# A selective-scan kernel on Trainium2: loops written out, softplus parts added on TensorE, five items read out by GpSimd, step rows replicated first

## The reference

```python
def mamba_block(seq, in_proj_w, conv_w, conv_b, x_proj_w, dt_proj_w, dt_proj_b, A_log, D, out_proj_w):
    xz = jnp.einsum('bld,ed->ble', seq, in_proj_w)
    u, z = jnp.split(xz, 2, axis=-1)
    ...
    u = jax.nn.silu(u)
    x_dbl = jnp.einsum('bld,ed->ble', u, x_proj_w)
    dt, Bm, Cm = jnp.split(x_dbl, [DT_RANK, DT_RANK + D_STATE], axis=-1)
    dt = jax.nn.softplus(jnp.einsum('blr,dr->bld', dt, dt_proj_w) + dt_proj_b)
    A = -jnp.exp(A_log)

    def step(h, inputs):
        dt_t, B_t, C_t, u_t = inputs
        dA = jnp.exp(dt_t[:, :, None] * A)
        h = dA * h + (dt_t * u_t)[:, :, None] * B_t[:, None, :]
        y = jnp.einsum('bdn,bn->bd', h, C_t)
        return (h, y)
    ...
    y = ys.transpose(1, 0, 2) + u * D
    y = y * jax.nn.silu(z)
    return jnp.einsum('bld,ed->ble', y, out_proj_w)
```

## Time and profile before

| | |
|---|---|
| median of 3 runs | 1939.89 us (1939.37 to 1941.07) |
| the profiled execution, its own time | 1938.45 us |
| its span | 1936.7 us |
| busy, share of the span | PE 80%, ACT 51%, DVE 66%, POOL 63% |
| DMA | 311.06 MB, mean 161 GB/s |
| scans of layer 0 (first to last gate) | 73.3 to 578.1 us |
| scans of layer 1 (first to last gate) | 1095.8 to 1602.2 us |

### The profile page before, as it was taken

The page is one execution under the profiler, slowest core; times in us unless marked ns, Lnnn a source line. Parts: engine busy times, 40 slices in busy tenths (PEclk is TensorE's granted clock), DMA queues, the critical chain, the costliest instruction groups (busy, mean ns, idle before and its releaser), DMA issues. The chain is left out here.

```text
span 1936.7 us, 25492 instructions
## 1 busy us (share of the span) xinstructions
PE 1546.9 (80%) x6220; PEld 927.2 (48%) x6221; DVE 1271.6 (66%) x2146; ACT 991.2 (51%) x1594; POOL 1211.5 (63%) x1179
## 2 busy tenths in 40 slices
PE   5677777777778998999982687777777777699996
PEld 3222222222228998989981222222222227566664
DVE  5799999999996531111115799999999996411012
ACT  4777777777772211222223777777777772122112
POOL 2699999999981001444435699999999992123310
PEclk8799999999995899999995799999999995599997
DMA  5788777787774204777765877788877881423313
GB/s 131 191 183 185 181 179 177 176 186 179 178 160 155 85 25 143 233 220 218 226 162 134 206 179 176 179 182 179 181 176 174 184 186 49 171 78 122 123 62 107
DMA packets 104507, 311.06 MB, mean 161 GB/s; under 512 B 19389, under 2 KB 74509, under 8 KB 93069
## 3 DMA queue, kind: packets, MB, share of 16 engines
q1 hardware_dynamic: 91896, 291.72, 60.1%
q0 software_dynamic: 12544, 18.63, 4.1%
HBM read 258.83 MB, written 51.45 MB: 160 GB/s over the span
## 5 line engine op out<-in xcount | busy, mean ns | idle before, releaser
L689 POOL TENSOR_TENSOR mamba_dbu<-mamba_rep 128x462 f32<-128x462 f32 x640 | 677.2, 1085 | 66.1 <-DMA mamba_rep<-dt_rows 66.1
L509 PE MATMUL mamba_ysum<-mamba_hc,all_sel 128*128 128x462 f32 x800 | 379.4, 588 | 148.3 <-DVE mamba_hc L797 147.3
L621 ACT ACTIVATE mamba_state<-mamba_rep,all_m_acol 128x462 f32<-128x462 f32 x640 | 388.9, 638 | 156.6 <-DVE mamba_last L808 155.6
L811 DVE TENSOR_TENSOR_SCAN mamba_state<-mamba_state,mamba_carry,mamba_dbu 128x462 f32<-128x462 f32 x400 | 455.4, 1179 | 0.0
L509 PEld LDWEIGHTS mamba_ysum<-mamba_hc,all_sel 128*128 128x128 f32 x800 | 130.3, 190 | 398.3 <-DVE mamba_hc L797 318.8
L808 DVE TENSOR_TENSOR_SCAN mamba_last<-mamba_state,mamba_last,mamba_dbu 128x462 f32<-128x462 f32 x240 | 280.3, 1168 | 15.2 <-POOL mamba_dbu L689 12.4
L684 POOL TENSOR_TENSOR mamba_hcp<-mamba_last,mamba_rep 128x462 f32<-128x462 f32 x240 | 266.7, 1111 | 5.6 <-DVE mamba_last L808 5.6
L504 PE MATMUL mamba_ysum<-mamba_hcp,all_sel 128*128 128x462 f32 x480 | 227.8, 570 | 50.1 <-POOL mamba_hcp L684 50.0
L797 DVE TENSOR_TENSOR mamba_hc<-mamba_state,mamba_rep 128x462 f32<-128x462 f32 (+1 forms) x240 | 230.7, 961 | 0.0
L1433 DVE TENSOR_TENSOR moe_h<-moe_sg,moe_up 128x512 f32<-128x512 f32 x62 | 42.6, 688 | 283.0 <-PE moe_up L1242 276.6
L504 PEld LDWEIGHTS mamba_ysum<-mamba_hcp,all_sel 128*128 128x128 f32 x480 | 85.3, 190 | 172.4 <-POOL mamba_hcp L684 119.6
(11 more groups left out here) (236 smaller groups left out, 2285.6 us busy)
## 6 DMA issues: line engine op xcount, KB each, us to landing
mamba_rep<-bc_rows SPq DMA_DIRECT2D x168, 462.0 KB, 7.4
mamba_rep<-dt_rows SPq DMA_DIRECT2D x168, 462.0 KB, 7.5
weights_wgu<-in_L_gu_dram SPq DMA_DIRECT2D x88, 512.0 KB
dt_rows<-mamba_dd SPq DMA_DIRECT2D x168, 115.5 KB, 7.2
weights_w<-in_L_w_dram SPq DMA_DIRECT2D x16, 1024.0 KB
mamba_xs<-seq_scratch SPq DMA_DIRECT2D x92, 116.0 KB, 9.2
seq_scratch<-mamba_y SPq DMA_DIRECT2D x40, 116.2 KB, 7.0
normed_rows<-xn SPq DMA_DIRECT2D x16, 288.0 KB, 7.1
```

The source lines that it names most:

```text
L509: nc.tensor.matmul(ysum[:, 0:TC], sel[:, i // NM, :], hc[:, n % HCD, :], start=False, stop=end).then_inc(hc_summed, 1)
L621: nc.scalar.activation(state[:, STATE_BANK[i], 0:TC], rep[:, par * REP_ROWS + i // NM, :], ACT.Exp, scale=m["acol"][:, i:i + 1]).then_inc( ...
L689: pool.tensor_tensor(dbu[:, i % 4, :], rep[:, first + NG + i // NM, :], rep[:, first + 2 * NG + i % NM, :], ALU.mult).then_inc(dbu_ready, 1)
L811: nc.vector.tensor_tensor_scan(bank, bank, dbu[:, i % 4, :], carry[:, i:i + 1], ALU.mult, ALU.add).then_inc(scan_done, 1)
```

## The change

- `ON_POOL` has five items, (1, 4, 7, 10, 13), for six. The buffers `hc` (now seven slots, by a table) and `hcp` (five for three) follow.
- The loops over the chunks of SP, PE and ACT, which ran in hardware loops, are written out; positions that were computed in registers are constants.
- Softplus: ScalarE writes the ln to `ab` in SBUF; TensorE adds ln, max(x, 0) and minus the correction in `front` with three matmuls against the identity and its negative (`prep_add`); ScalarE copies the sum into `dd` (`prep_dd`). VectorE's L720 and L726 go.
- SP: in the loop the order is store of `dd`, step rows, B and C rows, `bc` store, `xs`; `xs` is loaded one chunk further ahead, and `dt_rows` has two halves.
- The positions of the front end's steps among the items are others; `prep` on GpSimd stands after item 1 for item 3.

```diff
@@ -41,7 +41,7 @@
 UBUFS = 4
 BANKS = 5
-ON_POOL = (0, 3, 6, 8, 11, 13)
+ON_POOL = (1, 4, 7, 10, 13)
 ON_DVE = tuple(i for i in range(ITEMS) if i not in ON_POOL)
 NP_, ND = len(ON_POOL), len(ON_DVE)
 FIRST = tuple(i in ON_DVE and i + 1 in ON_DVE for i in range(ITEMS))
@@ -52,11 +52,13 @@
 STATE_GAP = tuple(min(n for n in range(1, ITEMS + 1) if STATE_BANK[i - n] == STATE_BANK[i]) for i in range(ITEMS))
 LAST_OF = tuple(i + 1 if FIRST[i] else i for i in range(ITEMS))
 SUM_ORDER = tuple(sorted(range(ITEMS), key=lambda i: LAST_OF[i] + 2 if i in ON_DVE else i + 3.1))
-HCP = 3
-HCD = 5
-
-
-AT_SILU, AT_EXP, AT_ONE, AT_LN, AT_BC, AT_DT, AT_DTU, AT_Y, AT_RR = 6, 10, 11, 15, 13, 3, 3, 2, 13
+HCP = 5
+HC_SLOT = (0, 1, 2, 3, 4, 5, 6, 1, 2, 3, 4)
+HC_GAP = tuple(min(d for d in range(1, ND + 1) if HC_SLOT[n - d] == HC_SLOT[n]) for n in range(ND))
+HCD = max(HC_SLOT) + 1
+
+
+AT_SILU, AT_EXP, AT_ONE, AT_BC, AT_LN, AT_U, AT_DTU, AT_Y, AT_RR, AT_ADD, AT_DD = 3, 6, 7, 8, 12, 9, 1, 2, 8, 7, 15
 START = 16
 NE, TOPK = 8, (2, 1)
 F0, F1 = 512, 1024
...
@@ -339,12 +332,13 @@
     def store_dt(k):
         sp.wait_ge(front_pool, START + k + 1)
+        half_rows = g["dt_rows"][bass.ds(k % 2, 1), :, :]
         for q in range(NG):
-            rows = g["dt_rows"].rearrange("(d w q) n -> q d w n", w=2, q=NG)[q]
+            rows = half_rows.rearrange("o (d w q) n -> q (o d) w n", w=2, q=NG)[q]
             sp.dma_start(rows, dd[q * DG:(q + 1) * DG, :, :]).then_inc(dt_stored, 16)
     def replicate_bc(k):
-        rows, row = bc_scratch(k), rep_row(k)
+        rows, row = bc_scratch(k), k % 2 * REP_ROWS
         sp.wait_ge(bc_stored, 16 * (k + 1))
         for s in range(NS):
             src = rows.rearrange("o (s w) n -> s (o w n)", s=NS)[s:s + 1]
...
@@ -402,28 +395,29 @@
         for c in range(CPB):
             store_seq(b, c)
     sp.wait_ge(seq_rest, 16 * RESTS)
+    sp.wait_ge(front_mm, START + MMS * 2 + MM_Z)
+    load_xs(3)
     tiles["room_free"](sp)
-    with sp.Fori(0, NCH) as k:
-        sp.reg_mul(replicas, k, 16 * REPS)
-        sp.reg_add(replicas, replicas, 16 * REPS)
-        replicas_before = sp.snap(replicas)
+    for k in range(NCH):
+        replicas_before = 16 * REPS * (k + 1)
         items_before = START + ITEMS * k
+        store_dt(k + 1)
         sp.wait_ge(decay_ready, items_before)
         sp.wait_ge(dbu_ready, items_before)
+        sp.wait_ge(rep_loaded, replicas_before)
+        replicate_dt(k + 1)
         sp.wait_ge(hc_ready, START + ND * k)
         sp.wait_ge(hcp_ready, START + NP_ * k)
-        sp.wait_ge(rep_loaded, replicas_before)
         replicate_bc(k + 1)
-        store_dt(k + 1)
-        replicate_dt(k + 1)
-        sp.wait_ge(front_mm, START + MMS * (k + 2) + MM_Z)
-        load_xs(k + 3)
         store_bc(k + 2)
+        sp.wait_ge(front_mm, START + MMS * (k + 3) + MM_Z)
+        load_xs(k + 4)
     sp.wait_ge(rep_loaded, 16 * REPS * (NCH + 1))
     sp.wait_ge(bc_stored, 16 * (NCH + 2))
-    sp.wait_ge(xs_loaded, 32 * (NCH + 3))
+    sp.wait_ge(xs_loaded, 32 * (NCH + 4))
+    sp.wait_ge(dt_stored, 16 * NG * (NCH + 1))
     if l == 0:
         sp.wait_ge(rows_zeroed, 1)
         zeros = hc[:, :, :].rearrange("p n c -> p (n c)")
@@ -448,16 +442,24 @@
                          start=False, stop=True).then_inc(front_mm, 1)
     def prep_z(k):
+        pe.wait_ge(front_act, START + ACTS * k)
         nc.tensor.matmul(front[:, 1, 0:TC], m["wz"][:, :], xs[:, 2:2 + TC],
                          start=True, stop=True).then_inc(front_mm, 1)
     def prep_dt(k):
         pe.wait_ge(front_act, START + ACTS * k + A_Z)
-        nc.tensor.matmul(front[:, 0, 0:TC], m["wdt"][:, :], chunk_of(pe, u, k),
+        nc.tensor.matmul(front[:, 0, 0:TC], m["wdt"][:, :], chunk_of(u, k),
                          start=True, stop=True).then_inc(front_mm, 1)
+    def prep_add(k):
+        pe.wait_ge(front_act, START + ACTS * k + A_LN)
+        nc.tensor.matmul(front[:, 1, 0:TC], g["ident"][:, :], ab[:, :], start=True, stop=False)
+        nc.tensor.matmul(front[:, 1, 0:TC], g["ident"][:, :], rx[:, :], start=False, stop=False)
+        pe.wait_ge(front_dve, START + DVES * k + D_R)
+        nc.tensor.matmul(front[:, 1, 0:TC], nident[:, :], rr[:, :], start=False, stop=True).then_inc(front_mm, 1)
+
     def prep_bc(k):
-        nc.tensor.matmul(front[0:2 * DS, 1, 0:TC], m["wbc"][:, :], chunk_of(pe, u, k),
+        nc.tensor.matmul(front[0:2 * DS, 1, 0:TC], m["wbc"][:, :], chunk_of(u, k),
                          start=True, stop=True).then_inc(front_mm, 1)
     for s in range(NT + LAG):
@@ -483,6 +485,8 @@
             prep_dt(0)
             prep_bc(0)
         if s == AT_U1:
+            pe.wait_ge(minus_ready, 1)
+            prep_add(0)
             prep_u(1)
             prep_z(1)
         if s == AT_DT1:
@@ -490,12 +494,14 @@
             prep_bc(1)
     if l == 0:
         tiles["tensor_weights"](pe, 1)
-    with pe.Fori(0, NCH) as k:
-        prep_u(k + 2)
-        prep_z(k + 2)
-
+    prep_add(1)
+    prep_u(2)
+    prep_z(2)
+    for k in range(NCH):
+        prep_dt(k + 2)
+        prep_bc(k + 2)
         pe.wait_ge(y_ready, START + k)
-        nc.tensor.matmul(ysum[:, 0:TC], m["diag"][:, :], chunk_of(pe, u, k), start=True, stop=False)
+        nc.tensor.matmul(ysum[:, 0:TC], m["diag"][:, :], chunk_of(u, k), start=True, stop=False)
         for at, i in enumerate(SUM_ORDER):
             end = at == ITEMS - 1
             if i in ON_POOL:
@@ -506,12 +512,13 @@
             else:
                 n = ON_DVE.index(i)
                 pe.wait_ge(hc_ready, START + ND * k + n + 1)
-                nc.tensor.matmul(ysum[:, 0:TC], sel[:, i // NM, :], hc[:, n % HCD, :],
+                nc.tensor.matmul(ysum[:, 0:TC], sel[:, i // NM, :], hc[:, HC_SLOT[n], :],
                                  start=False, stop=end).then_inc(hc_summed, 1)
-            if at == AT_DT:
-                prep_dt(k + 2)
-            if at == AT_DT + 1:
-                prep_bc(k + 2)
+            if at == AT_ADD:
+                prep_add(k + 2)
+            if at == AT_U:
+                prep_u(k + 3)
+                prep_z(k + 3)
     pe.wait_ge(front_dve, START + DVES * (NCH + 2))
     for t in range(NT):
...
@@ -565,11 +564,17 @@
     def prep_ln(k):
         act.wait_ge(front_act, START + ACTS * k + A_BC)
-        nc.scalar.activation(front[:, 1, 0:TC], ex[:, :], ACT.Ln, bias=1.0).then_inc(front_act, 1)
+        nc.scalar.activation(ab[:, :], ex[:, :], ACT.Ln, bias=1.0).then_inc(front_act, 1)
+
+    def prep_dd(k):
+        act.wait_ge(front_mm, START + MMS * k + MM_ADD)
+        if k > 0:
+            act.wait_ge(dt_stored, 16 * NG * k)
+        nc.scalar.activation(dd[:, 0, :], front[:, 1, 0:TC], ACT.Copy).then_inc(front_act, 1)
     def prep_bc(k):
         act.wait_ge(front_mm, START + MMS * k + MM_BC)
-        if not (isinstance(k, int) and k == 0):
+        if k > 0:
             act.wait_ge(bc_stored, 16 * k)
         nc.scalar.activation(bc[:, :], front[0:2 * DS, 1, 0:TC], ACT.Copy).then_inc(front_act, 1)
@@ -598,14 +603,16 @@
         if s == AT_DT0:
             prep_rest(0)
         if s == AT_U1:
+            prep_dd(0)
             prep_silu(1)
         if s == AT_DT1:
             prep_rest(1)
+    prep_dd(1)
     if l == 0:
         tiles["scalar_weights"](act, 1)
     act.wait_ge(placed, 2 * NT)
     nc.scalar.preload_act_table_set("exp_and_others")
-    with act.Fori(0, NCH // 2) as pair:
+    for pair in range(NCH // 2):
         for par in range(2):
             k = pair * 2 + par
             act.wait_ge(rep_loaded, 16 * REPS * (k + 1))
@@ -620,6 +627,8 @@
                     act.wait_ge(hc_ready, START + ND * k + ON_DVE.index(LAST_OF[free]) + 1 - ND * before)
                 nc.scalar.activation(state[:, STATE_BANK[i], 0:TC], rep[:, par * REP_ROWS + i // NM, :], ACT.Exp,
                                      scale=m["acol"][:, i:i + 1]).then_inc(decay_ready, 1)
+                if i == AT_DD:
+                    prep_dd(k + 2)
                 if i == AT_SILU:
                     prep_silu(k + 2)
                 if i == AT_EXP:
@@ -714,17 +723,6 @@
         nc.vector.scalar_tensor_tensor(out=rr[:, :], in0=front[:, 0, 0:TC], scalar=1.0, in1=ex[:, :],
                                        op0=ALU.subtract, op1=ALU.subtract).then_inc(front_dve, 1)
-    def prep_ln(k):
-        dve.wait_ge(front_act, START + ACTS * k + A_LN)
-        dve.wait_ge(front_dve, START + DVES * k + D_R)
-        nc.vector.tensor_tensor(front[:, 1, 0:TC], front[:, 1, 0:TC], rr[:, :], ALU.subtract).then_inc(front_dve, 1)
-
-    def prep_dt(k):
-        if not (isinstance(k, int) and k == 0):
-            dve.wait_ge(dt_stored, 16 * NG * k)
-        dve.wait_ge(front_dve, START + DVES * k + D_LR)
-        nc.vector.tensor_tensor(dd[:, 0, :], front[:, 1, 0:TC], rx[:, :], ALU.add).then_inc(front_dve, 1)
-
     def statistics(t):
         dve.wait_ge(ready, t + 1)
         nc.vector.bn_stats(stats[:, t, :], T[:, t, :]).then_inc(sstat_steps, 1)
```

(13 more changed lines are left out.)

54 lines of the change are left out of this document (19 added, 35 removed).

## The result

The changed kernel takes 2040.84 us (median of 4 runs, 2038.99 to 2042.44) against 1939.63: ratio 1.0521, 95% interval 1.0503 to 1.0539. The forecast was slower, by 50 us; it is slower by 101. The profiled execution takes 2038.99 us, its span is 2037.0.

The account below looks back on a forecast made before the run. The rows' DRAM round trip, made serial, was to bound the scans: 3.2 + 4.2 + 19.3 = 26.7 us a chunk, +1.3 over 18 periods a layer, about +25 us per layer, +50 in all: 1990 us, range 1946 to 2034.

Parts of the forecast that it names:

- The mechanism: Scan loops: dd stores, step rows, then B and C rows run serially, 26.7 us a chunk, longer than VectorE's 24.4.
- Landed to first store: Each chunk, from rep landed to the first dd store: two dbu and prep on GpSimd, 3.2 us.
- Stores on an empty queue: Each chunk, the four dd stores with no traffic ahead, first issue to release: 4.2 us, for 8.8 behind B and C rows.
- Step rows and then B and C rows: Each chunk, both replications: 11.3 us plus 8.0 us at 237 GB/s, 19.3 us, bounds 17.7 and 20.9.
- The base: Period of a chunk before the change, 25.39 us; the forecast trip of 26.7 us adds 1.3 us to it.
- case C: Replication pair: xs and bc rows interleave with it, pair 20.9 us, period 28.3, +107 us, 2047 us; chance 0.08.
- Case A: Scan loops: pair under 17 us, so the trip stays under VectorE's loop; ScalarE decides, period 24.7, 1917 us; chance 0.14.
- Case B: Scan loops: trip at its lower bound, 25.3 us, only the prologue's loss remains, 1940 us; chance 0.06.
- Case D: TensorE at its lower clock, 1.2 GHz, becomes the bound: 25 matmuls take 38 us, 2100 us and more; chance 0.02.
- ScalarE and writing out: Chunk loops: an added Copy and moved table load hidden under waits; written-out loops worth nothing, at most 0.1 us a chunk.
- Outside the scans: Prologue: three matmuls +4.6 us, earlier normalisation -2.4, through the seq stores about +2 us, bounds 0 and 5.
- Last chunk: Each layer's last chunk ends on VectorE and is 0.5 us shorter.

Follow-up runs that it names:

- the kernel with thin rows: The changed kernel with seven of the eight B and C rows left out of the replication from chunk 2 on; 1926.95 us, ratio 0.9931.
- the old order: The changed kernel with SyncE's issue order of before (B and C rows, dd stores, step rows); 1939.59 us, ratio 0.9977.
- the stores ahead: The changed kernel with prep at the end of the chunk before, order stores, B and C rows, step rows, and silus one item later; 1919.65 us, ratio 0.9904.

## Why the prediction was slower by half only

- **The mechanism: right.** The order of the issues makes the trip serial, and the trip is the period: 36 of the periods carry 92.3 of the 100.3 us ((27.92 - 25.35) and (27.99 - 25.43), times 18 each).
- **Landed to first store, 3.2 us: right** (3.18). **Stores on an empty queue, 4.2: nearly** (4.42; each lands 2.3 us after its issue, where 2.22 was read from the earlier trace rows). 36 x 0.2 = 8 us.
- **Step rows and then B and C rows, 19.3 us: this step failed.** The prediction took 8.0 us for the second replication, from one microsecond at 237 GB/s; the pair is 20.35. By the landings in the trace the step rows are through after 11.3 us, as forecast, and the B and C rows 9.0 us after them; the kernel with thin rows puts the full second replication at 9.4. The upper bound of the step, 20.9, with "the step rows' slower pace" for both, was the nearer end, and the lower rate stood in the trace of before (223 and 203 GB/s over a replication). 36 x 1.05 = 38 us.
- **The base, 25.39.** The sum gave 26.7, and 27.95 is 1.25 above it: 36 x 1.25 = 45 us, nearly all of the miss.
- **The range failed in a step of its own.** The sum's bounds were 24.9 to 28.3; the forecast's range stopped at 27.8 and the rest was left to case C with its chance of 0.08. 28.3 alone gives 36 x 2.9 + 3 = 107 us, the figure of case C. A bound that came from a row belonged inside the range. The working isn't consistent here either: the chances name a trip of 25.5 to 27.8 us, the range is worked out with +0.2 to +2.2 us, that is 25.6 to 27.6, and the lower bound by its own terms is 3.2 + 4.2 + 17.7 = 25.1, not 24.9.
- **Case C: its number was right and its reason was not.** It rested on `xs` interleaving with the pair; moving `xs` from the end of the pair to its head changed nothing (1.0504 against 1.0521).
- **Case A: refuted as a forecast, confirmed as a mechanism.** It needed the pair in under 17 us, and the pair takes 20.35. But with the transfers out of the way ScalarE does hold item 4, and the chunk is 24.84 us, 0.1 from the 24.7 worked out there. VectorE's own loop, put at 24.4, is 24.54. The Trainium skill, "DMA: Bandwidth & Descriptors", section "Anatomy of one DMA — SWDGE (gpsimd) path", gives about 2.0 us plus the bytes at 436 GB/s for a DMA that GpSimd issues; as an estimate by that page's figure, the pair would take some 11 us. These DMAs are issued by SyncE, so it isn't the page's own case, and the trace is far from it: the best microsecond of the 19 moved 251 GB/s, and the pair took 20.35 us.
- **Case B: no.** It needed a trip at its lower bound of 25.3 us.
- **Case D: no.** TensorE was never the bound; see below.
- **ScalarE and writing out, "nothing": wrong.** On the kernel before it is a gain of about 0.2 us a chunk. The prediction read the wait at the chunk's head as one on GpSimd; but GpSimd's first product was through at 271.9, and ScalarE's first exponential, behind its table load, only at 272.8, 0.2 us before the scan: the 2.8 us of waiting lie ahead of that load and hide nothing of it. In the changed kernel no load stands at the head at all, as the prediction said (it comes before item 13, since `AT_LN` is 12 for 15). The trip there runs from the landing through GpSimd and SyncE and not through ScalarE, so I argue that nothing of the gain is left.
- **Outside the scans: +2.4 before the first gate, forecast +2; +3.1 between the layers and +2.1 at the end, where +2 and 0 stood.** In layer 0 the size was luck: the chain named, through the stores of `seq`, did not hold. Those stores go out 1.2 us earlier than before, and the first scan starts later because ScalarE stands 4.90 us for `prep_add(1)`, the three added matmuls of chunk 1, before it can load its table and make the first exponential (row below). Between the layers the expert stage, with the same code, is 3.4 to 5.8 us longer in the changed kernel and the seven built on it (in the changed kernel 270.3 us from the first of its 84 weight loads to the next layer's first load, for 264.5 before), and 2.8 us longer in the kernel before with the new order alone. Neither the written-out loops (264.4) nor the size of the scratch tensors (264.2) does it by itself. What does stays open, and so does the end's +2.1, on which no experiment was made.

```profile
67.43 0.56 ACT L573 ACTIVATE mamba_dd<-mamba_front 128x462 f32<-128x462 f32 x1 [4.90 <-PE mamba_front L459]
```

- **Last chunk, -0.5: right** (22.70 for 23.15). The first chunk, 25.5 as before, is right in layer 0 (25.37) and 1.2 us too low in layer 1 (26.73).

## What to carry to other kernels

Where a chunk's data make a trip through DRAM that is as long as the compute loop, write the trip as a sum of issues, landings and waits before reordering a queue: an order that starts one transfer earlier can put a wait in front of all of them. Take a transfer's rate as the mean over its whole length, not from the best microsecond, and keep every bound that a row supports inside the range. Once a wait is gone, the next limit here lay 0.1 to 0.3 us below (ScalarE at one item, then the trip again: 25.17, 24.84, 24.76 and 24.58 us a chunk from the old order to the stores ahead), so most of a gain on paper needed more edits before it showed.

## What the runs showed of the hardware

- Four stores of 116 KB on an empty queue are through 4.42 us after the first issue; behind the B and C rows they take 8.8. Four more DMAs for the same bytes (B and C rows apart) didn't lengthen a chunk: 24.84 us, where VectorE and ScalarE bound it.
- The same source line has ScalarE's table load, 1.28 us, behind the wait for the rows in the loop and ahead of it written out. With SyncE's and TensorE's loops written out beside it this is worth 0.5% of the time.
- TensorE restarts slowly in each chunk. It stood 4.95 us before the first matmul here; the granted clock of the next microseconds is 0.50, its lower level of 1.2 GHz, then 0.92 and 1.00. Two matmuls take 1.91 us for the 0.94 that the same shape has later on. Windows and timeline of the kernel after:

```profile
269.00:270.00 1.00, 1.00 (x2) 0.18 (x2) 1.00 (x2) 1.00 (x3) 1.00 (x3) 0.50 0.57 129
272.00:273.00 1.00, 1.00 (x4) 0.60 (x3) 1.00 (x2) 1.00 (x3) 1.00 (x2) 0.92 1.06 251
...
267.50 1.91 PE L451 MATMUL mamba_front<-mamba_u,all_m_wdt 128*128 128x462 f32 x2 [4.95 <-ACT mamba_sz L550]
...
272.44 0.94 PE L515 MATMUL mamba_ysum<-mamba_hc,all_sel 128*128 128x462 f32 x2
```

I see no cost of it: the kernel with the stores ahead has such waits too (120.9 us, 40 times), and its chunk is VectorE's own 24.54 us all the same.
